# One step less lead for the inflow, scatters one to a unit, and list and block-input sum moved in GpSimd's table

## What is computed

```python
# block: x is layernorm(input)
xc = silu(conv1d(ln(x) @ in_proj[:256].T)); z = ln(x) @ in_proj[256:].T
dt, B, C = split(xc @ x_proj.T)            # 8, 16, 16 columns
delta = softplus(dt @ dt_w.T + dt_b)
dA  = exp(delta[..., None] * -exp(A_log))  # (b, l, 256, 16)
dBu = delta[..., None] * B[:, :, None] * xc[..., None]
h = dA_t * h + dBu_t;  y_t = sum_n h * C_t # over the 2048 steps
x = x + ((y + xc * D) * silu(z)) @ out_w.T
x = x + silu(gate) * val @ ffp_w.T + ffp_b # gate, val of ln(x)
# around it
x = input + x
x = x + sum_k w_k * expert_k(layernorm(x)) # top 2 of 8 experts, 344 wide
```

## Time and profile before

| | us |
|---|---|
| median of 3 runs (lowest, highest) | 851.82 (850.19, 853.87) |
| the profiled execution | 846.1 |
| its span, first to last instruction | 844.3 |
| first scan, last scan (start) | 44.9, 700.5 |

### The profile page before, as it was taken

One profiled execution on the slowest core, in us unless ns is written; L12 is line 12 of the kernel. 1 busy time (PEld: TensorE's weight loads), 2 busy tenths in 40 slices (PEclk: granted clock), 3 DMA queues, 4 the chain that ended last, 5 costly groups with the idle time before them and its releaser, 6 DMA issues.

```text
span 844.3 us, 12617 instructions
## 1 busy us (share of the span) xinstructions
PE 649.8 (77%) x3545; PEld 465.3 (55%) x3545; DVE 739.2 (88%) x1145; ACT 506.5 (60%) x1091; POOL 581.2 (69%) x487
## 2 busy tenths in 40 slices
PE   4438688878778877887877876886876789888991
PEld 2124445545355536764566635873554457788990
DVE  1376998989999999999999999999999897686774
ACT  2545795876688577464846577555854775444440
POOL 1094675677977797689958896789846994456451
PEclk9659899989989898997989988897887899999995
DMA  6923233223323336542464336532424621123247
GB/s 175 263 104 103 87 113 113 82 84 97 116 69 107 106 102 182 158 145 99 130 174 140 109 96 203 148 110 94 133 91 128 171 61 33 39 65 83 65 129 231
DMA packets 80248, 99.94 MB, mean 118 GB/s; under 512 B 10215, under 2 KB 48051, under 8 KB 80163
## 3 DMA queue, kind: packets, MB, share of 16 engines
q1 hardware_dynamic: 75859, 90.21, 36.3%
q0 software_dynamic: 4320, 8.92, 3.0%
HBM read 87.56 MB, written 15.35 MB: 122 GB/s over the span
## 4 chain that ended last, share of the span: by engine, by line
DVE 37%; PE 34%; issue 17%; ACT 7%; DMA 2%; POOL 2%; DVEq 1%; SPq 0%; ACTq 0%; POOLq 0%
DVE state L1077 18%; PE work_front L1248 4%; PE y L1288 4%; DVE product L1087 4%; PE up L1399 2%; PE work_front L1254 2%; PE y L1284 2%; PE up L1410 2%; PE gate L1392 2%; DVE stats L1007 2%; ACT decay L941 1%; DVE silu_m L1213 1%; PE gate L1313 1%; DVE arena L1052 1%; PE work_side L1332 1%
## 5 line engine op out<-in xcount | busy, mean ns | idle before, releaser
L818 POOL TENSOR_TENSOR inflow<-du,b_wide 128x1024 f32<-128x1024 f32 x128 | 315.5, 2468 | 145.0 <-DVE product L1087 92.0
L1077 DVE TENSOR_TENSOR_SCAN state<-decay,carry,inflow 128x512 f32<-128x512 f32 x192 | 234.7, 1264 | 6.5 <-ACT decay L941 6.5
L1087 DVE TENSOR_TENSOR product<-state,c_wide 128x1024 f32<-128x1024 f32 (+1 forms) x93 | 139.1, 1495 | 4.4 <-PE y L1284 3.3
L941 ACT ACTIVATE decay<-arena,a_neg 128x512 f32<-128x512 f32 x128 | 86.6, 688 | 60.7 <-DVE state L1077 56.9
L1284 PE MATMUL y<-ident,product 128*128 128x128 f32 x664 | 106.4, 305 | 20.6 <-DVE product L1087 20.5
L1284 PEld LDWEIGHTS y<-ident,product 128*128 128x128 f32 x664 | 87.2, 158 | 62.5 <-issue 34.7
L848 POOL DMA_INDIRECT y_dram<-y_rows,x_rows x71 | 82.5, 1162 | 56.0 <-ACT y_rows L997 49.1
L941 ACT ACTIVATE decay<-delta_odd,a_neg 128x512 f32<-128x512 f32 x128 | 86.6, 689 | 56.3 <-DVE state L1077 56.1
L1288 PE MATMUL y<-h_rows,ident 128*128 128x512 f32 x180 | 100.9, 652 | 7.0 <-ACT h_rows L906 6.5
L842 POOL DMA_INDIRECT row_dram<-m_tok,place x64 | 74.4, 1163 | 24.3 <-issue 12.7
L1077 DVE TENSOR_TENSOR_SCAN state<-decay,inflow 128x512 f32<-128x512 f32 x64 | 74.5, 1203 | 6.1 <-ACT decay L941 3.6
(11 more groups left out here) (232 smaller groups left out, 1342.6 us busy)
## 6 DMA issues: line engine op xcount, KB each, us to landing
b_wide<-bc_dram SPq DMA_DIRECT2D x128, 256.0 KB, 3.3
c_wide<-bc_dram SPq DMA_DIRECT2D x93, 256.0 KB, 3.5
w_stage<-gate_up_dram SPq DMA_DIRECT2D x26, 344.0 KB, 4.2
x_rows<-row_dram SPq DMA_DIRECT2D x71, 65.0 KB, 1.9
arena<-gate_up_dram SPq DMA_DIRECT2D x8, 344.0 KB, 4.4
x_tok<-in_x SPq DMA_DIRECT2D x8, 256.0 KB, 5.8
out<-x_tok SPq DMA_DIRECT2D x8, 256.0 KB, 4.8
inflow<-y_dram SPq DMA_DIRECT2D x6, 256.0 KB, 4.4
```

What stands on the lines that cost most here:

```text
L818: e.tensor_tensor(inflow[:, key % 3], du[:, c % 2], b_wide[:, key % ROW_SLOTS:key % ROW_SLOTS + 1, :].to_broadcast([P, HALVES, CHUNK]), AL ...
L941: e.activation(decay_bank[h][:], delta[c % 2][:, h, :], ACT.Exp, scale=a_neg[:, h, n:n + 1]).then_inc(S["decay"], 1)
L1077: e.tensor_tensor_scan(state[:, key % STATE_SLOTS, h, :], decay_bank[h][:], inflow[:, key % 3, h, :], 0.0 if c % (SEQ // CHUNK) == 0 else ...
L1087: e.tensor_tensor(product[:, key % 2, :, :wide], state[:, key % STATE_SLOTS, :, :wide], c_wide[:, key % ROW_SLOTS:key % ROW_SLOTS + 1, :wi ...
```

## The change

- An inflow of unit key waits for the product of unit key - 2, or, where that unit has no product, for its scans. Before it was key - 3.
- In SEND the eight scatters stand one to a unit in n = 0 to 7, tag1 in n = 4; list0 in n = 6, list1 in n = 8, list2 in n = 9. Before there were two scatters at n = 0, 1, 3 and 5, with the lists at n = 2, 6 and 7. SEND_HELD is as it was.
- x_sum stands in the row of n = 8 of BACK instead of that of n = 7.
- A chunk enters `sent` with its last scatter and `listed` with list2. So load_x of a round's first tiles is put ahead of list2, from n = 8 on, and load_w from n = 10 on; before, both from n = 8 on.

```diff
@@ BACK
     (("n_turn",), ("n_t",), ("ff_gate",)),
-    (("x_sum",), ("gate_h",), ("ff_val",)),
-    ((), ("silu_g", "ff_h"), ("ff_out",)),
+    ((), ("gate_h",), ("ff_val",)),
+    (("x_sum",), ("silu_g", "ff_h"), ("ff_out",)),
     ((), ("x_four", "stats3"), ()),
@@ SEND
-    ("tag0", ("scatter", 0, 0), ("scatter", 1, 0)),
-    (("scatter", 2, 0), ("scatter", 3, 0)),
-    ("list0",),
-    ("tag1", ("scatter", 0, 1), ("scatter", 1, 1)),
-    (),
-    (("scatter", 2, 1), ("scatter", 3, 1)),
+    ("tag0", ("scatter", 0, 0)),
+    (("scatter", 1, 0),),
...
+    (("scatter", 2, 1), "list0"),
+    (("scatter", 3, 1),),
     ("list1",),
     ("list2",),
@@ send(), in plan()
                 put(name, key)
+                if name == "scatter" and key[1:] == (SUB - 1, TOPK - 1):
+                    sent.add(key[0])
                 if name == "list2":
-                    sent.add(key)
                     listed.add(key)
@@ inflow, on POOL
-                    if key >= 3:
-                        if share[key - 3] < SUB:
-                            e.wait_ge(S["times_c"], products[key - 3])
+                    if key >= 2:
+                        if share[key - 2] < SUB:
+                            e.wait_ge(S["times_c"], products[key - 2])
                         else:
-                            e.wait_ge(S["scan"], HALVES * (key - 2))
+                            e.wait_ge(S["scan"], HALVES * (key - 1))
```

## The result

The changed kernel takes 894.45 us (median of four runs, 892.12 to 895.16), the kernel before, run beside it, 852.51 (850.19 to 853.87): a ratio of 1.0494, interval 1.0475 to 1.0513. It is 42 us slower, where 34.5 were forecast. An instruction is called **stretched** where its row lasts longer than others of its kind, and an inflow **locked** where it waited for a product and so starts at that product's end.)

The account below looks back on a forecast made before the run. VectorE (DVE) was taken to set the time in the scanning part, work or wait. Losses in chunks 1 to 7 summed to 34.5 us, added to the 851.8 us median for 886.3 us; range 858 to 906.

Parts of the forecast that it names:

- the walk: Chunk 5 stepped through by instruction prices and port waits, giving starts of inflows and scans; chunk loses 6.9 us.
- product 82: Chunk 5: DVE's product stretched 2.34 us before, 0.5 after, with inflow 83 instead of 84 over it.
- half product 84: Chunk 5: DVE's half product stretched 2.42 us before, 0.95 after.
- shift2: Chunk 5, unit 85: DVE's shift loses 2.5 us before, 3.65 after, since inflow 86 and then rstd2 end late.
- x_four: Chunk 5, unit 89: waits 2.3 us for x_sum, now behind inflow 90; at least 1.5 in chunks 1 and 2.
- the series: Chunk 5: DVE's series on the lists waits 1.05 us, as inflow 91 ends that long after its wanted start.
- shift3: Chunk 5: DVE's shift, ready at 521.2, waits 3.4 us for rstd3, behind list2 and inflow 92, until 524.6.
- the round's gate: Chunk 5: late tile_i delays weights, so moe_h of unit 92 waits 1.3 to 3 us; 1.4 taken.
- Chunk 4: Loses 3.4 us: its own collisions are reset by the change, set against scans 0.12 us shorter per pair.
- That waits stay small and collisions go: Rival, whole kernel: POOL keeps time, 46 us of stretches go and 22 of waits come; 828 us, chance 0.11.
- The port that costs POOL less: Rival: adds and scatters take 1.0 us throughout, so 12 to 18 us of loss remain; 866 us, chance 0.14.
- That little changes: Rival: DVE and POOL find another phase with collisions costing as much; 848 to 856 us, chance 0.05.

Follow-up runs that it names:

- the wait alone: Kernel before with only the inflow's wait moved to unit key - 2; SEND, x_sum and loads as before: 891.13 us, 1.0452.
- the tables alone: Changed kernel with the old wait (key - 3); SEND tables, x_sum and loads' order moved: 860.41 us, 1.0105.
- x_sum early: Changed kernel with x_sum back in the row of n = 7: 890.15 us, 1.0438 against the kernel before.
- the port kernel: Separate kernel computing none of the reference, pairing VectorE and GpSimd instructions: product 1.23 us alone, 3.14 under an inflow; DMA 1.04, held 1.44 or 1.72.
- the last pair of kernels: Kernel before with weight slots 5 to 4 and row slots 8 to 7: 848.83 us; the same with fourth inflow buffer, wait key - 4: 887.19.
- its control: Kernel before with four instead of five weight slots and seven instead of eight row slots, three inflow buffers: 848.83 us, 1.0033.

## Why the prediction was right, and where it was off

**The bound and the mechanism** held. DVE sets the time, a wait on it is the kernel's, and both engines lose at the port as the walk had it.

**Chunk 5, by the walk.** Forecast 6.9, measured 6.85 (99.71 less 92.86, between first scans). Inflows 82 to 90 were forecast at 460.6, 466.45, 472.2, 477.4, 482.6, 490.35, 494.3, 500.85 and 505.35; on that clock they started at 461.4, 467.4, 473.0, 479.4, 484.4, 491.9, 495.8, 502.2 and 506.6. By terms, forecast and measured: product 82 0.5 and 0.24; half product 84 0.95 and 0; shift2 3.65 and 3.53; product 86 2.0 and 1.70; products 87 and 88 2.6 and 2.28; x_four 2.3 and 2.31; the series 1.05 and about 0.2; shift3 3.4 and 2.86; the round's gate 1.4 and 2.3. The sum also hides an omission: in n = 2 and 3 DVE waits 2.6 us in all for tanh_m and work_side (1.18 in the row at 500.25), which the walk had at nothing. The terms that came out smaller paid for it. Each term is right to about 1 us; that their sum fits to 0.05 is luck. Two readings behind it were off. DVE's periods in n = 2 and 3 were given as 3.5 and 5.3 us and are 4.5 and 6.4 in the trace before, since moe_h (1.1) also runs there; the walk's own scan starts have it in. And "at least 1.7" for shift2's wait doesn't follow from its sum, 3.9 to 4.2 less 2.37, which gives 1.5 to 1.8: the shortest, in chunk 1, was 1.50.

**The wait and the tables.** What the walk had wrong is which part of the change costs what. It puts the wait's share of chunk 5, the terms up to product 89, at 9.7 after against 10.9 before, a gain of 1.2, and the whole loss on x_sum, the lists and the gate. Each alone, the wait costs that chunk 6.2 us and the tables 0.6. The reason is in the rows: with the wait alone shift2 waits 5.34 in chunk 5 and a scan 2.41 for its inflow, where in the changed kernel shift2 waits 3.53 and no scan does; with the tables alone x_four and shift3 wait as in the changed kernel, but the stretches of product 82, half product 84 and shift2, 7.2 us before, are gone without the wait's help. The prediction booked that gain to the wait. The total stands, since it was walked for both together; what it said of the wait as such does not.

**x_sum and the lists.** The forecast had 1.5 in two chunks and 2.3 in four, 12.2; the table has 12.4 in 6. But only 4.3 of it is time: with x_sum early, other waits take its place. So a wait's size was forecast well, and what its removal returns is another number.

**The gate.** Forecast: tile_i written at 519.5, the weights issued 6.5 us later, and 1.3 to 3 us of wait, 1.4 taken. Tile_i is written at 519.5 on the old clock (a POOL row that ends at 543.72), the rows' load is issued at 544.83, which is 520.6, 14.4 later than 506.23, and the first weights at 548.85, 5.1 after tile_i; the wait is 2.3:

```profile
544.83 0.34 SPq L767 DMA_DIRECT2D x_rows<-row_dram  x1
...
548.85 2.03 SPq L746 DMA_DIRECT2D w_stage<-gate_up_dram  x3
...
553.39 1.62 PE L1395 MATMUL gate<-x_cols,w_stage 128*128 128x128 f32 x6 [6.07 <-DMA w_stage<-gate_up_dram]
```

**The other chunks.** Forecast 0, 3.2, 4.2, 6.8, 3.4, 6.9, 6.9, 3.1 for chunks 0 to 7; measured -0.9, 4.3, 6.8, 4.3, 7.4, 6.85, 6.5, 5.0, together 40.3 for 34.5. Chunk 4 is the term that was mis-sized most: I let the change reset its own collisions, so that it would end up like chunk 5, less its shorter scans. It kept all its surplus (101.7 against 99.7 us). Chunk 3 came 2.5 under its term and chunk 7 1.9 over; no run here says why. Chunks 1 and 2 differ by 3 us between two profiles of the same kernel, so only their sum can be held against the forecast: 7.4, measured 11.1.

**The tail** was put at nothing, since its order is kept, and is 5.2 us longer. Every kernel with an edit has 145.6 to 149.0 there, the unchanged one 142.5 and 143.1. Its slices of 20 us show a lower granted clock of TensorE in places (0.89 at 60 to 80 us behind the last scan). Before, all slices but the last stand at 1.00, so within the tail the clock may be part of the difference; but the second profile of the unchanged kernel has 0.91 in that slice with a tail of 143.1. The cause is open.

**The step from profile to median** added 5.7 us to the forecast. The profile before was below its median (846.1 to 852.5), the one after is not (893.76 to 894.45), so the 47.7 us between the profiles are 42 between the medians, and the forecast of +34.5 was 7.4 short. The 42 are made up of 40.3 in the chunks, for 34.5, and of a start 2.2 and a tail 5.2 longer, both put at nothing, less the 5.7 of this step.

**The rivals.** That waits stay small and collisions go was wrong on the waits, and mostly on the collisions: products did lose 14 us of their 36 (of 31.8 in the second profile of the kernel before, 9), a third rather than all. The port that costs POOL less is refuted by the port kernel. That little changes, 848 to 856, is refuted by the time. The Trainium skill (SBUF — State Buffer, "Who interferes with whom") holds in these rows for the inflow and the two-SBUF product; its inference that a tensor_tensor leaves descriptor generation alone doesn't fit the rows of L131 and L142, where the DMA takes 1.44 and 1.72 us instead of 1.04. These DMAs also read their row numbers from SBUF, and which part of them stands still no run here shows.

**Lead** explains the changed kernel as far as the walk goes: the inflows of chunk 5 started within 2 us of the forecast that lateness gives. It isn't a measure of time, as I had taken it to be before the last pair of kernels: one unit less is 4.5% slower, but so is one more, by another way of losing. The release by the product three behind leaves 40 inflows starting where only scans follow, and yet keeps POOL ahead; the release two behind locks 45 but leaves what stands behind them late; four behind locks 25, and many of the others fall on two-input instructions. That total loss goes with how the inflows' starts lie against these is my reading of the traces; no experiment moved the starts alone. The count of locked inflows isn't the rule: the wait alone has 46 and its products still lose 36 us, the tables alone 47 and lose 20, and the kernel before has 40. Which of order and phase would make two or four behind as good was not tried.

## What to carry to other kernels

Where two engines share a port, a buffer's release is also a clock: it decides under which instruction the other engine's work falls. Here both a stricter release and one more buffer cost 4.5%. Before a producer's wait is made stricter, list what stands behind it in its queue and who wants each of these in the next unit: here a root of 1.4 us behind a late inflow made VectorE wait 3.5. A collision or a wait that is removed is a gain only if the next two-input instruction doesn't inherit it; walk the queues forward through a whole stage, since the waits in the table were some three times what their removal returned (36.6 us for 10.6, 12.4 for 4.3). And check what else an edit of a table moves: two of these kernels had six half products fewer on VectorE, which no line of their edit says.

## What the runs showed that I hadn't expected

- An indirect DMA of GpSimd stands still for a VectorE product of two SBUF inputs that started before it (1.44 and 1.72 us against 1.04 alone), and in the other order neither is held (1.08 and 1.20 us).
- With the tables alone two of the changed kernel's waits are there at full size (2.31 and 2.87 us), and the chunk is only 0.6 us longer.
- Taking four-element instructions off VectorE made the kernel 0.65% slower.
- A fourth buffer made it 4.9% slower, 4.5% beside its control, with VectorE busy 99% of chunk 5.
